# Graph network kernel: the last layer's running base moved from TensorE to VectorE, and the edge layer's count products spread over three PSUM banks

## The reference

```python
h = relu(layernorm(x)); x = x + L0(h)      # edge layer: per edge relu([x_i, x_j - x_i] @ W1 + b1) @ W2 + b2, maximum per destination
h = relu(layernorm(x)); x = x + L1(h)      # norms from both degrees, sum over the edges, one matrix
h = relu(layernorm(x)); x = x + L2(h)      # two hops of the mean over the incoming edges
h = relu(layernorm(x)); x = x + L3(h)      # last layer: see below

def _L3_gnn_ref(x, edge_index, edge_weight, W_self, b_self, W_neigh, b_neigh, num_nodes):
    row, col = (edge_index[0], edge_index[1])
    message = x[col] * edge_weight[:, None]
    neigh_agg = jax.ops.segment_sum(message, row, num_segments=num_nodes)
    return x @ W_self.T + b_self + neigh_agg @ W_neigh.T + b_neigh
```

## Time and profile before

| | us |
|---|---|
| median of 3 runs | 15991.63 (15991.48 to 16015.87) |
| the profiled execution | 16003.64, span 16001.9 |

### The profile page before, as it was taken

The page is one execution under the profiler, slowest core; times in us unless marked ns, Lnnn a source line. Parts: engine busy times, 40 slices in busy tenths (PEclk is TensorE's granted clock), DMA queues, the critical chain, the costliest instruction groups (busy, mean ns, idle before and its releaser), DMA issues. The chain is left out here.

```text
span 16001.9 us, 222885 instructions
## 1 busy us (share of the span) xinstructions
PE 7367.6 (46%) x68791; PEld 5151.8 (32%) x68791; DVE 8618.9 (54%) x11890; ACT 6120.9 (38%) x10705; POOL 7519.5 (47%) x7085
## 2 busy tenths in 40 slices
PE   1155555555555555559979999920000000000055
PEld 1144444444444444425545555510000000000045
DVE  5276766666666766754444434344444444444475
ACT  0133333333333333347767777722222222222201
POOL 4455555555555555431101111166666666666600
PEclk9955555555555555579989989955555555555588
DMA  6333333333333333346646656622222222222186
GB/s 257 141 117 119 121 115 114 114 115 115 115 115 115 115 115 115 104 131 204 204 141 204 200 157 204 183 59 56 55 57 57 58 55 57 57 55 59 47 303 233
DMA packets 1622964, 1983.23 MB, mean 124 GB/s; under 512 B 513958, under 2 KB 1419271, under 8 KB 1617498
## 3 DMA queue, kind: packets, MB, share of 16 engines
q1 hardware_dynamic: 1302057, 1257.39, 26.8%
q10 hardware_dynamic: 94032, 435.46, 6.6%
q0 software_dynamic: 226176, 281.93, 6.3%
HBM read 1171.70 MB, written 816.17 MB: 124 GB/s over the span
## 5 line engine op out<-in xcount | busy, mean ns | idle before, releaser
L644 POOL DMA_INDIRECT RF<-tab_edge_b,idx x3125 | 3417.5, 1094 | 2837.1 <-DMA idx<-e_src 1830.2
L1207 POOL DMA_INDIRECT records<-RF,idx x3125 | 3095.0, 990 | 1591.2 <-issue 990.3
L697 DVE TENSOR_TENSOR HM<-iota_b,eqw 128x2048 bf16<-128x2048 bf16 x2000 | 2193.1, 1097 | 1723.5 <-PE bk L1977 1027.4
L1817 ACT ACTIVATE X<-bk 128x392 uint8<-128x392 f32 x4000 | 1852.5, 495 | 2879.9 <-PE bk L1977 1619.2
L1977 PE MATMUL bk<-HM 128*128 128x98 bf16 x16000 | 1718.5, 267 | 2677.2 <-issue 1547.1
L1977 PE MATMUL kp<-HM,ident_b 128*128 128x98 bf16 x3125 | 275.3, 282 | 4377.2 <-DVEq L1726 2575.9
L1977 PEld LDWEIGHTS bk<-HM 128*128 128x128 bf16 x16000 | 1192.8, 124 | 3199.1 <-issue 3116.0
L781 PE MATMUL tp<-HM,RF 128*64 128x512 bf16 x12276 | 2003.3, 379 | 6.1 <-DVE HM L742 1.1
L881 POOL DMA_INDIRECT agg<-RF,lastT x372 | 528.5, 1421 | 2864.3 <-ACT RF L820 2773.5
L1977 PEld LDWEIGHTS kp<-HM,ident_b 128*128 128x128 bf16 x3125 | 251.7, 141 | 4401.7 <-issue 4401.7
L787 PE MATMUL om<-HM,RF 128*64 128x512 bf16 x6138 | 1451.4, 379 | 0.0
(11 more groups left out here) (375 smaller groups left out, 14032.2 us busy)
## 6 DMA issues: line engine op xcount, KB each, us to landing
dst_f<-counts SPq DMA_DIRECT2D x465, 512.0 KB
RF<-first_rows SPq DMA_DIRECT2D x250, 800.0 KB
counts<-X ACTq DMA_DIRECT2D x250, 784.0 KB
RF<-records SPq DMA_DIRECT2D x220, 784.0 KB, 5.1
records<-pivots SPq DMA_DIRECT2D x120, 1400.0 KB
crow<-counts SPq DMA_DIRECT2D x279, 512.0 KB
first_rows<-RF ACTq DMA_DIRECT2D x25, 4000.0 KB
edge_rows<-RF ACTq DMA_DIRECT2D x125, 800.0 KB
```

The lines of the kernel that those rows point to most:

```text
L644: e.indirect_dma_start(out=ring[:, r, j, :], out_offset=None, in_=table[:, :], in_offset=bass.IndirectOffsetOnAxis(ap=idx[:, r, own(j):own ...
L697: return e.tensor_tensor(to[:, 0:n, :].rearrange("p k (q h) -> p k q h", h=2), iota_b[:, 0:m].rearrange("p (q h) -> p q h", h=2).unsqueeze ...
L1207: e.indirect_dma_start(out=records[:, :], out_offset=bass.IndirectOffsetOnAxis(ap=idx2[:, r, j:j + 1], axis=0), in_=msgs[MSG_OF[r]][:, j, ...
L1817: e.activation(staged[u].rearrange("p (r k) -> p r k", k=P)[:, :, k:k + 4], bk[s % 2][:, 0:4 * TILES].rearrange("p (k r) -> p r k", k=4), ...
```

## The change

The running base: TensorE's loop of the last layer (25 products in each block, with the semaphores `looked` and `based`) is gone. VectorE sums the one-hots over the block's 25 columns itself, into the 128 x 98 tile `stat["tmp"]`, and adds that to `base`, which stays in PSUM. The order on VectorE is otherwise the same, and it no longer waits ahead of L697.

The count products: the four products of number j now go to `count_banks[j % 3]`, which are `bk[0]`, `bk[1]` and `tp[1]`. TensorE may begin those of j when ScalarE has copied out those of j - 3. `tp[1]` no longer takes transposes: all four groups q use `tp[0]`, so `turn` waits until the group before has been copied out.

```diff
+        count_banks = (bk[0], bk[1], tp[1])
+        def bank_last(j):
+            return max(g for g in range(CW) if g % 3 == j)
...
+            in_block = stat["tmp"][:, :]
...
-                    wait(e, "based", b)
-                    gate(e)
                     loop_chain(row_onehots(e, oh_lane, rtwice[:, :, :], TILES))
                     loop_chain(e.tensor_tensor(at, oh_lane, base.unsqueeze(1).broadcast_to([P, K, TILES]), ALU.mult))
-                    e.sem_inc(sem("looked"), 1)
-                    loop_chain(e.tensor_reduce(out=atbase[:, :], in_=at, op=ALU.add, axis=AX.X))
+                    e.tensor_reduce(out=atbase[:, :], in_=at, op=ALU.add, axis=AX.X)
+                    loop_chain(e.tensor_reduce(out=in_block, in_=oh_lane.rearrange("p k q -> p q k"), op=ALU.add, axis=AX.X))
+                    loop_chain(e.tensor_tensor(base, base, in_block, ALU.add))
...
-            e.wait_ge(sem("based"), BLOCKS)
...
-                                 bk[s % 2][:, 0:4 * TILES].rearrange("p (k r) -> p r k", k=4), ACT.Copy)\
+                                 count_banks[(v * 4 + s) % 3][:, 0:4 * TILES].rearrange("p (k r) -> p r k", k=4), ACT.Copy)\
...
-                    e.activation(hT[0:rows, q % 2, 0:w], tp[q % 2][0:rows, 0:w], ACT.Relu)\
+                    e.activation(hT[0:rows, q % 2, 0:w], tp[0][0:rows, 0:w], ACT.Relu)\
...
-                    wait(e, "bank_out", b * CW + (v * 4 + s - 1))
+                    j = v * 4 + s
+                    wait(e, "bank_out", b * CW + (j - 2 if j > 2 else bank_last(j) + 1 - CW))
...
-                        last = whole(bk[s % 2][:, m * TILES:(m + 1) * TILES], ohq[v % 2][:, s * 4 + m, :],
+                        last = whole(count_banks[j % 3][:, m * TILES:(m + 1) * TILES], ohq[v % 2][:, s * 4 + m, :],
...
-                wait(e, "copied0", b * NQ + (q - 1))
+                wait(e, "copied0", b * NQ + q)
...
-            def body4(i):
-                for r in range(R):
-                    wait(e, "looked", i * R + (r + 1))
-                    gate(e)
-                    for j in range(K):
-                        last = whole(base, ident_b[:, :], oh_lane[:, j, :], False, j == K - 1)
-                    last.then_inc(sem("based"), 1)
-            loop(e, body4)
```

More of the change, by code:

```diff
@@ L2005, in turn @@
                     m = len(c) * D
-                    last = e.transpose(tp[q % 2][0:m, k * P:(k + 1) * P],
+                    last = e.transpose(tp[0][0:m, k * P:(k + 1) * P],
                                        ring[:, r, c[0]:c[-1] + 1, :], ident[:, :])
```

## The result

Changed kernel: 15,757.5 us median (15,702.1 to 15,773.0), kernel before beside it 16,002.2 us (15,991.5 to 16,015.9): ratio 0.984, 95% interval 0.981 to 0.987. It is faster by some 245 us. The profiled execution has a span of 15,767.0 us, 234.9 less than that of before. Forecast were 371 us less.

The account below looks back on a forecast made before the run. The prediction took GpSimd's writes, pausing for VectorE held by TensorE's late semaphore, to bound the last layer; 296 us there plus 75 us in the edge layer, 371 us less, gave 15,620 us, range 15,200 to 15,870.

Parts of the forecast that it names:

- The removed wait: Last layer: without VectorE's wait for TensorE's base products, 25 long blocks end 14.3 us earlier on average, 358 us together.
- The added sum: Last layer, VectorE: strided sum 4.24 us plus addition 0.26 us; 27 fast blocks pay, half of 124 us taken, 62 us.
- The forecast was -296: Last layer in total: 358 us won less 62 us for the added sum, 296 us, with bounds of 234 and 358.
- this balance: Last layer: GpSimd's pauses and the slow stretches of late completions keep each other in balance; no size of its own.
- The third bank: Edge layer: count products start without waiting for a copy, 0.6 us in each of 125 blocks, 75 us.
- The single transpose bank: Edge layer: transposes wait for the previous group's copy, cost 0; without cover 1 us once in a block.
- The bound of 895 us: Edge layer: TensorE's total wait for banks to be copied out, the upper bound of gain if all lay on the path.
- (a): Last layer: without TensorE's instructions ScalarE gets faster and GpSimd never pauses, 601 us instead of 296, 15,315 us; chance 25%.
- (b): Edge layer: completions come a fixed time late, so three banks take 523 us off VectorE's waits, 15,172 us; chance 8%.
- (c): Last layer: VectorE meets the wait at its next instruction, the sum adds 304 us, slower at 16,221 us; chance 9%.
- (d): Both layers: the balance settles where it was and the edge layer gives nothing, no change at 15,990 us; chance 8%.

Follow-up runs that it names:

- e6: Changed kernel with eight more ACTIVATEs on ScalarE in each last-layer block, into an unread PSUM bank: 15,773.7 us, 0.985 of the kernel before (16,013.8 us on that chip).
- e4: Changed kernel with the base's strided sum on VectorE computed twice in each last-layer block: 15,706.6 us, 0.980 of the kernel before (16,013.8 us on that chip).
- e2: Kernel before with only the third count bank and single transpose bank, TensorE's base products kept: 13,715.0 us against 13,756.5 us, ratio 0.997.
- e7: Changed kernel with one count bank in the edge layer instead of three: 17,902.0 us, 1.117 of the kernel before (16,013.8 us on that chip).
- e3: Changed kernel plus 25 TensorE products of constants in each last-layer block that nobody waits for: 0.9991 of the kernel before on the same chip.
- e10: Repeat of e3, meant for a chip where the kernel before takes about 16,000 us, but run on a faster one: 0.9984 of the kernel before there.
- e8: Changed kernel with the base's sum done by contiguous additions of halves instead of one strided sum: 15,752.4 us, 0.984 of the kernel before (16,013.8 us on that chip).

## Why the prediction was right, and where it wasn't

The range and the sign held. Forecast were 371 us less for the profiled execution, 235 came.

**The removed wait: right.** 25 blocks of 61.4 us were to become 14.3 us shorter each, with ScalarE late next at 38 us. No block is over 56 us now; those of 40 to 56 us take 47.2 us on average: (61.4 - 47.2) x 25 = 355 us, against 358. The wait moved to L1740, the group still takes 38 us. e6 shows the rate for an instruction behind it.

**The added sum: its size was right (4.39 and 0.27 us against 4.24 and 0.26), its place in the sum was not.** I let 41 short blocks pay and hid 14 of them and half of the rest, 62 us. All of them show it: 42 short blocks x 4.4 us = 185 us. Against that stands a term that I didn't have: there are six long blocks (over 40 us) fewer, 51 and not 57, and four short ones and two of 24 to 40 us more, 4 x (47.2 - 22.2) + 2 x (47.2 - 33.4) = 128 us. The remaining 60 us are slightly longer blocks in the two middle classes. -355 + 185 - 128 + 60 = -238, by blocks; -221 by the writes. The forecast was -296. That the two lie this near is partly luck: the sum cost 123 us more than I had given it, and the term that I didn't have brought back 128.

The step that failed is thus not a single price but the adding of prices. GpSimd's pauses end ScalarE's late stretches, and late stretches make the pauses; I named this balance and then summed as if blocks were independent. e4 and e6 measure it: 550 us more of VectorE cost nothing, 255 us more of ScalarE's groups 66. What changed one engine's time in these runs moved the number of long blocks too.

**The third bank: right in kind, its size open on the late chip.** The pair of traces gives 0.28 us a block instead of 0.6, the other traces of the same edge layer up to 0.79, so 0.6 can't be called wrong there; e2 finds 0.22 on a prompt chip. The single transpose bank cost nothing that can be seen: it is part of e2, which is faster. The bound of 895 us from TensorE's waits was far too wide; e7 shows what a hand-over costs that nothing hides, 16 us a block; with two banks nearly all of it was hidden already.

**The rivals.** (a) ScalarE gets faster without TensorE's instructions: refuted, 38.2 us with TensorE at rest. Its full-length groups (34 us and more) are 37 after and 33 before; but late stretches seem to begin later behind a pause: two short blocks in a row are common after, one was the rule before. Whether that is TensorE's absence or VectorE's longer block is open; e3 and e10 were to tell and met chips without lateness. e4, with longer blocks still, has the fewest full groups (29), and e8, whose short blocks are 0.8 us shorter, the most (59), which speaks for the block's length; but e7, with the last layer of the changed kernel, has 32 and not 37, and the kernel before, with the shortest blocks of all, has 33, so length alone doesn't explain it. (b) A delay instead of a rate in the edge layer: it asked for 523 us there, and the traces give 35 to 99. (c) VectorE meets the wait anyway: refuted, 4.3 us ahead of L702, and a long block waits some 25 us in all (47.2 - 22.2), under the 40 that the rival needed. (d) was half true: the balance gives back, but not all.

**What nobody had forecast** is that the premise of the whole sum, completions at 1.3 us each in a burst, isn't there on three of the chips. I had one trace, and took what it shows for a trait of the program. On the prompt chips the forecast would have been wrong by all of its main term.

What makes the one chip late isn't settled. The traces show that it is tied to GpSimd's bursts, goes by instructions, spares VectorE and ends with a pause; they don't show what the completions wait for. In the edge layer it is worth more than this change: the gathers take 6,317 us on the late chip and 4,793 on a prompt one.

## What to carry to other kernels

Before a wait is priced, ask whether it exists on another chip: a wait whose records don't add up (2.2 us of products, 64 us until the semaphore) may be a trait of the chip, and a second profile settles it sooner than any sum. A second profile also gives the spread of a stage: 64 us between traces of the same edge layer, more than the 35 us that one pair of traces gave the third bank. Where two engines hold each other in balance, the block-by-block sum gives the sign and a bound, and the size needs a run in which one of the times is doubled. On VectorE beside GpSimd's indirect writes, a slow sum with one source can be cheaper than a fast tree of additions with two.

## What was not expected of the hardware

- Chips of the same type differ by 16% on the same kernel: 16,013.8 us on one, 13,752.8 to 13,763.7 us on three others. Most of it lies in the two stages with GpSimd's bursts of indirect transfers: gathers 6,317 against 4,793 us, writes of before 4,659 against the 4,061 of e2, where that layer is as before; GpSimd's step from one write to the next is 1.3 us on both.
- On the late chip ScalarE's completions in a burst come at 1.32 us for an instruction, for 29 as for 37 of them, while VectorE's next steps follow at once.
- A strided sum of 2,450 bf16 elements takes 4,394 ns, 1.79 ns for an element. The three largest additions of the same sum by halves take 1,383, 770 and 465 ns, but lengthen GpSimd's write beside them from 0.97 to 1.50 us, once in each block.
